# One more unit per reflection step, the grid's count one batch later, and a new order of ScalarE's slot, in a graph-network layer with attention

## The reference

```
h = relu(layernorm(x))                     # per node, over 1024 features
U = eigenvectors of the Laplacian of adj   # 120 x 120, once for all batches
agg = U^T h;  hid = relu(agg @ W1 + b1)    # 1024 -> 128
out = hid @ W2 + b2                        # 128 -> 1024
f = softmax(theta(out)^T maxpool(phi(out)))# attention over the 1024 positions
z = BN(wo(f @ maxpool(g(out)))) + out
result = x + U z + z
```

## Time and profile before

| | |
|---|---|
| median of 3 runs | 3321.01 us (3320.54 to 3321.21) |
| profiled execution | 3320.95 us |
| its span, first to last instruction | 3319.2 us |
| busy, whole span | PE 3169.2, DVE 2316.4, ACT 2407.8, POOL 1884.4 us |
| last reflection's `zs` (L1045) | 441.96 us |
| first matmul of the attention (L827) | 632.19 us |
| chain that ended last, by engine | PE 81%, DVE 10%, ACT 5%, issue 4% |

### The profile page before, as it was taken

How to read it: one execution, slowest core, us unless ns; L and a number is a source line. 1 busy time by engine, 2 the same in 40 slices (tenths; PEclk the granted TensorE clock), 3 DMA queues, 4 the chain that set the end, 5 groups by cost and what they waited for, 6 DMA issues and landing times.

```text
span 3319.2 us, 65434 instructions
## 1 busy us (share of the span) xinstructions
PE 3169.2 (95%) x16040; PEld 2544.0 (77%) x16040; DVE 2316.4 (70%) x6363; ACT 2407.8 (73%) x4380; POOL 1884.4 (57%) x1722
## 2 busy tenths in 40 slices
PE   6888987799999999999999999999999999999997
PEld 4677776577777777777777777777777777777775
DVE  8998888766666666666666666666666666666664
ACT  6889999666666666666666666666666666666665
POOL 3222212166666666666666666666666666666665
PEclk9999999899999999999999999999999999999998
DMA  3333444222222222222222222222222222222222
GB/s 101 92 101 108 111 113 113 61 61 72 72 72 72 72 72 72 72 72 72 72 72 72 72 72 72 72 72 72 72 73 72 74 72 72 72 72 72 72 72 66
DMA packets 111582, 256.28 MB, mean 77 GB/s; under 512 B 47500, under 2 KB 49797, under 8 KB 111493
## 3 DMA queue, kind: packets, MB, share of 16 engines
q1 hardware_dynamic: 111493, 255.25, 27.7%
HBM read 190.69 MB, written 63.44 MB: 77 GB/s over the span
## 4 chain that ended last, share of the span: by engine, by line
PE 81%; DVE 10%; ACT 5%; issue 4%; POOL 0%; DMA 0%; DVEq 0%; POOLq 0%; ACTq 0%; SPq 0%
PE ps_M L811 8%; PE ps_M L813 8%; PE ps_M L812 8%; PE ps_S L888 7%; PE ps_E L811 7%; PE ps_O L811 7%; PE ps_E L812 7%; PE ps_O L813 7%; PE ps_O L812 7%; PE ps_E L813 7%; PE ps_M L872 3%; ACT P L544 2%; ACT P L534 1%; ACT fT L551 1%; PE ps_S L893 1%
## 5 line engine op out<-in xcount | busy, mean ns | idle before, releaser
L508 POOL TENSOR_TENSOR p_lo<-p,p_hi 128x512 fp32r<-128x512 f32 x1024 | 1374.9, 1343 | 942.1 <-ACT p_hi L663 938.1
L658 ACT ACTIVATE p<-ps_E 128x512 f32<-128x512 f32 x1024 | 614.1, 600 | 331.9 <-PE ps_E L813 307.3
L1423 DVE TENSOR_REDUCE nmx<-ps_S 128x1 f32<-128x512 f32 x1024 | 658.8, 685 | 130.7 <-PE ps_S L888 126.7
L663 ACT ACTIVATE p_hi<-p 128x512 fp32r<-128x512 f32 x1024 | 647.1, 632 | 32.6
L811 PE MATMUL ps_E<-o_hi,Q_hi 123*128 123x512 f32 x1024 | 426.9, 417 | 0.0
L811 PE MATMUL ps_O<-p_hi,v_hi 128*121 128x512 f32 x1024 | 406.2, 397 | 4.1 <-POOL p_lo L508 4.1
L813 PE MATMUL ps_O<-p_lo,v_hi 128*121 128x512 f32 x1024 | 406.3, 397 | 0.0
L812 PE MATMUL ps_E<-o_hi,Q_lo 123*128 123x512 f32 x1024 | 404.7, 395 | 0.0
L812 PE MATMUL ps_O<-p_hi,v_lo 128*121 128x512 f32 x1024 | 404.5, 395 | 0.0
L813 PE MATMUL ps_E<-o_lo,Q_hi 123*128 123x512 f32 x1024 | 403.7, 394 | 0.0
L1403 DVE TENSOR_REDUCE gf<-ps_M 128x256 f32<-128x512 f32 x256 | 177.1, 692 | 262.7 <-PE ps_M L813 262.7
(11 more groups left out here) (364 smaller groups left out, 5953.2 us busy)
## 6 DMA issues: line engine op xcount, KB each, us to landing
rbc<-r_dram SPq DMA_DIRECT2D x128, 484.0 KB
xin<-in_x_dram SPq DMA_DIRECT2D x128, 480.0 KB, 4.1
xt<-in_x_dram SPq DMA_DIRECT2D x128, 480.0 KB, 4.9
out_dram<-y SPq DMA_DIRECT2D x128, 480.0 KB, 3.7
o_hi<-mrow SPq DMA_DIRECT2D x256, 2.0 KB
dcol<-y SPq DMA_DIRECT2D x128, 4.0 KB, 2.0
r_dram<-rcol SPq DMA_DIRECT2D x128, 4.0 KB, 1.4
W1s<-in_L_gnn_W_dram SPq DMA_DIRECT2D x1, 512.0 KB, 4.1
```

The costliest lines, as they stand in the source:

```text
L508: pool.tensor_tensor(p_lo[:, c % 4, :], p[:, c % 4, :], p_hi[:, c % 4, :].bitcast(F32), ALU.subtract).then_inc(plo_sb, 1)
L658: act.activation(p[:, c % 4, :], ps_E[c % 2][:, :], ACT.Exp).then_inc(p_sb, 1)
L663: act.activation(p_hi[:, c % 4, :], p[:, c % 4, :], ACT.Copy).then_inc(phi_sb, 1)
L1423: dve.tensor_reduce(nmx[:, c:c + 1], ps_S[SBANK[c]][:, :], AX.X, ALU.max, negate=True).then_inc(max_sb, 1)
```

## The change

It has four parts. The steps get 10 units, not 9, for the first 60 steps after step 2 (`units_by`). `GRID_AT` goes from 102 to 103. In ScalarE's slot, `b_ft(k-2)` moves ahead of `b_relu(k)`, except in the last slots. The splits of W2 and Qw on VectorE move ahead of the wait for Z's transpose (`pe_out` 5).

```diff
             def slot(k):
                 par = k % 2
-                if k < B:
+                if k < B - 1:
+                    if k >= 2:
+                        b_ft(k - 2, par)
                     b_relu(k, par)
-                if k < B - 1:
                     b_sq(k, par)
-                if 0 <= k - 2 < B:
-                    b_ft(k - 2, par)
-                if k == B - 1:
-                    b_sq(k, par)
+                else:
+                    if k < B:
+                        b_relu(k, par)
+                    if k - 2 < B:
+                        b_ft(k - 2, par)
+                    if k < B:
+                        b_sq(k, par)
                 if k + 1 < B:
                     act.wait_ge(sq_done, k + 1)
                     b_sum(k + 1, 1 - par)
...
-                wanted = max(0, (k - LN_LEAD) * LN_RATE[0] // LN_RATE[1])
+                wanted = units_by(k)
                 reflect(k, done, wanted)
...
-            dve.wait_ge(pe_out, 5)
-            dve.tensor_copy(VT[:, :], ps_up[0:N, 0:N]).then_inc(dve_out, 1)
             def split(hi, lo, full):
                 step(dve.tensor_copy(hi, full))
                 mark(T(lo, full, hi.bitcast(F32), ALU.subtract))
-            i_hi = did(dve.tensor_copy(W2hi[:, :], W2f[:, :]))
+            split(W2hi[:, :], W2lo[:, :], W2f[:, :])
+            split(Qwhi[:, :], Qwlo[:, :], wn[:, 0, :])
+            dve.wait_ge(pe_out, 5)
+            dve.tensor_copy(VT[:, :], ps_up[0:N, 0:N]).then_inc(dve_out, 1)
             dve.wait_ge(pe_out, 6)
             mark(dve.tensor_copy(Uaug[0:N, :], ps_up[0:N, 0:N]))
             T(Cop[0:N, 2 * H + 1:OPS], ps_up[0:N, N:2 * N], ident[0:N, 0:N], ALU.add).then_inc(dve_out, 1)
-            need(i_hi)
-            mark(T(W2lo[:, :], W2f[:, :], W2hi[:, :].bitcast(F32), ALU.subtract))
-            split(Qwhi[:, :], Qwlo[:, :], wn[:, 0, :])
...
-LN_RATE, LN_LEAD, LN_BEHIND = (9, 1), 2, 3
-GRID_AT = 102
+LN_LEAD, LN_BEHIND, LN_LONG = 2, 3, 60
+def units_by(k):
+    steps = max(0, k - LN_LEAD)
+    return 9 * steps + min(steps, LN_LONG)
+GRID_AT = 103
```

## The result

The changed kernel takes 3310.05 us in the median of 7 runs (3308.99 to 3312.20), the kernel before 3320.61 (7 runs). The ratio is 0.9967, with a 95% interval of 0.9957 to 0.9978: 10.6 us faster, where 12.7 were forecast; the median lies 1.75 us above the forecast of 3308.3. The profiled execution took 3309.7 us, its span 3307.9, 11.3 less than before; L827, which is L831 now, starts at 621.71 instead of 632.19, 10.5 earlier. (From some lines on, the numbers are 2 or 4 higher than in the listing of before.)

The account below looks back on a forecast made before the run. L827, the attention's first matmul, sets the result: VectorE goes on 14.2 us earlier at the count, less 1.5 for the bare splits, so L827 is 12.7 us earlier; 3321.0 - 12.7 = 3308.3 us, range 3304 to 3314.

Parts of the forecast that it names:

- Ten units: Up to 443 us: the extra unit, 0.26 us a step, fits TensorE's idle time before L729; nothing taken for it.
- ScalarE's slot: New order: the mean waits for the square, slot 4.29 to 4.41 us; late loads add 0.06, giving 4.47 where ScalarE binds.
- When ScalarE is the bound: A slot of 4.47 us binds from 364.56 us on; slot 75 starts near 366.3, slot 93 near 446.8.
- TensorE's line: End of the first part: rectify 127 at 603.8 plus 9.0 us, so TensorE is free at 612.8, ahead of VectorE.
- the 615 that was named as a sign of error: Sign of being wrong: TensorE's last product ends after 615 us.
- the 2.5 that were named: Sign at the count: VectorE's idle time before L1202 is under 2.5 us.
- The splits: Between L1351 and the copy of Z's transpose: 2.4 us lie bare on VectorE, 0.9 won back, 1.5 us lost.
- ScalarE's line: Rival: slots of 4.60 us from longer loads, TensorE free at 619.6, 8 us gained, 3313 us; chance 0.22.
- The steps didn't stretch: Rival: the extra unit costs each of sixty steps 0.26 us, 15.6 us go back, 3321 to 3323 us; chance 0.10.
- Everything fits: Rival: the mean's wait is hidden and VectorE goes on at 495.95; 13.6 us gained, up to 3305.5 us; chance 0.12.
- the slow one: Rival: loads bound ScalarE throughout, slot 4.95 us, 18 us more than the ScalarE-last rival, 3331 us; chance 0.05.
- 2 us either way: Attention behind L827: TensorE starts it at half clock and the slow stretch may sit differently, 2 us either way.

Follow-up runs that it names:

- count-alone run: The kernel before with the grid's count at batch 99 instead of 102 and nothing else: 3319.63 us, ratio 0.9999.
- first experiment: The kernel before with ten units in the first sixty steps and the count at batch 103 only, ScalarE's slot and the splits as before: 3306.51 us, ratio 0.9961.
- third buffer: The changed kernel with a third buffer for x, so that a load goes out when square k-3, not k-2, is done: 3308.5 us (one run).
- forty-eight steps: The kernel before with ten units in 48 steps, the count at 102, slot and splits as before: 3304.77 us, ratio 0.9959; second run 3305.25 us, ratio 0.9953.

## Why the prediction was right

**The bound and the sum.** L827 sets everything, VectorE comes last with the splits bare, and the gain is what VectorE's wait at the count gives back less the splits. That held: 12.7 us forecast, 10.5 measured at L827 and 10.6 in the medians. The 2.2 us at L827 are 1.7 that the count came later than forecast and 0.6 from L1348 to L831 (8.07 against 7.5), less 0.1 in between. The count-alone run (nothing gained) shows that batches had to be moved too, and the first experiment that they and the count carry the whole gain.

**Ten units.** Taken at nothing. Right, and for the reason given: TensorE's idle time ahead of `zs` fell by 14.2 us, close to 60 units of 0.26. The 0.5 us at the seventh step that the profile shows is within what executions of the same steps differ by.

**ScalarE's slot.** The bare slot was forecast at 4.41 us and is 4.43. The loads were put at 0.06 us per slot. They hold it by 0.10 in the slots 75 to 93 (4.53 - 4.43), but by 0.07 over all 52 slots up to 127, and by 0.05 when the kernel was run again; the third buffer gives back 0.08 a slot. So the term was right over the whole, though it came from loads that nobody waited for, of median 4.1 us (4.2 in the changed kernel, 3.8 to 4.8).

**When ScalarE is the bound.** This is the step that was off. Forecast from 364.56 on. In the trace, ScalarE waits for TensorE only four times after slot 39, 0.2 us each: with ten units a step it is nearly full from 204 us on. The forecast let it begin slot 75 on time, at 366.3; it began at 367.53, 1.2 us late (0.8 in the repeated run). With 1.1 us more than forecast over the eighteen slots behind it, slot 93 began at 449.05 instead of 446.8. That is 2.25 us late, and at the count 1.7 are left of it (L1206 at 498.62, forecast 496.9): L1348 comes at 613.64 against 612.0.

**TensorE's line.** Its last product ended at 615.84, past the 615 that was named as a sign of error; the forecast was 612.8. Of the 3.0 us, 2.25 are the late slot 93. A slip in the forecast adds 0.9: it set rectify 127 at the start of slot 127, as in the old order, but the two copies stand ahead of it now. (Its sum also gives 604.0, not 603.8; the slots from 93 to 127 took 0.3 us less than forecast.) From there to the last product it was 8.97 us, as forecast. VectorE came last all the same, since the late slots held the count too, so both lines moved together; of the 2.2 us forecast between Z's transpose and its copy 1.2 were left. To that extent the right number owes something to errors that went the same way in both lines. VectorE's idle at the count, 2.55 us, is also a shade over the 2.5 that were named.

**The splits.** Forecast 1.5 us, measured 2.1 where VectorE comes last. The 0.9 us that `Cop` should have won back were 0.4 (from the copy of Z's transpose to L1368 2.77 us, before 3.21): TensorE's two products ahead of it took 0.61 and 0.62 us instead of 0.48 and 0.38, at a granted clock of 0.60 in the stretch from 618.8 to 619.9.

**ScalarE's page of the Trainium skill** (ScalarE: Activation LUTs, What ACT_TABLE_LOAD costs) gives 93 ns for the overlap of activations back to back; that one which waits for its forerunner loses just this was the prediction's own step. The slot grew by 0.14 us (4.43 against 4.29), and the gap behind the read from 0.09 to 0.24. The loss is larger here than the page's figure; the measurement decides.

**The rivals.** ScalarE's line didn't come last, though it came nearer than forecast. The steps didn't stretch. "Everything fits" failed at both of its conditions, and the slow one was never near.

## What to carry to other kernels

Where two engines' lines meet at a barrier (a point that needs both), shorten both and no more than that: a wait taken from one alone comes back at the meeting point, as the count at 99 showed (15.7 us turned into 14.8). Before an operation is moved ahead of another, look at what stood between two that depend on each other: the copies between square and mean hid a wait and gave a load almost 1 us of room, and moving them cost about 0.2 us in each slot where ScalarE was the bound, for nothing that a run here shows. A part of a change that only fills an idle time belongs behind the wait that it fills, not ahead of it: where VectorE came last, the moved splits cost 2.1 us. And before a difference of 1 us between two profiles is explained, look whether it was there before the change could act, as at the seventh step here.

## What the runs showed of the hardware

In the changed kernel TensorE's granted clock has fallen to half (1.2 GHz) before the attention starts, while it waits for VectorE behind the last products. Busy times and granted clock (the third number from the end) from 618 to 632 us:

```profile
618.00:632.00 14.00, 8.37 (x22) 5.38 (x21) 5.06 (x12) 2.02 (x4) 0.00 (x0) 0.54 0.00 0
```

Before the change it was still whole (1.00) from 630 to 632, up to L827, and 0.51 from 632 to 634; L827 itself takes 0.78 us in both. In the first experiment, where TensorE has idled 4.52 us ahead of L781, it is 0.51 from 612 to 620, and the two products L785 and L786 take 0.72 and 0.61 us, against 0.44 and 0.37 with all four parts. So part of what an early end of TensorE's work gives is lost in the short chain that closes the first part.

The slower slots of ScalarE did the same earlier on. In the changed kernel the clock is 0.63 from 598 to 600 and 0.51 from 600 to 602, behind an idle time of TensorE of 2.07 us (1.52 in the slot before); ScalarE had just waited 0.58 us for a late load. TensorE made that up before the end. With all but the splits it fell at 607.5, behind 2.44 us of idle time and a load 0.95 us late, in the last batches, and there it wasn't made up.

Behind L827 the forecast allowed 2 us either way. From L827 to the end of the span it is 2687.0 us before, 2686.2 after, 2684.8 in the first experiment, 2689.1 with all but the splits and 2683.5 in the first run of the forty-eight steps (2685.5 in the second). So it was a little more than 2 us at times, up to 3.5, and it scatters in the same kernel by 2.0; none of this is explained.
